# Inverted residual, odd blocks: second depthwise set ahead of the preceding block's output matmuls

## What is computed

```python
def _L3_conv_ref(x, w1, g1, b1, m1, v1, wd, gd, bd, md, vd, w2, g2, b2, m2, v2):
    HID, OUP = (288, 48)
    ...
    h = jnp.einsum('oc,bchw->bohw', w1, x)
    h = jax.nn.relu(_bn(h, g1, b1, m1, v1))
    h = jax.lax.conv_general_dilated(h, wd, window_strides=(1, 1), padding=((1, 1), (1, 1)), feature_group_count=HID, dimension_numbers=('NCHW', 'OIHW', 'NCHW'))
    h = jax.nn.relu(_bn(h, gd, bd, md, vd))
    h = jnp.einsum('oc,bchw->bohw', w2, h)
    h = _bn(h, g2, b2, m2, v2)
    return x + h
```

## Time and profile before

| what | before |
|---|---|
| median of 3 runs | 2010.66 us |
| range of the runs | 2002.27 to 2011.61 us |
| the profiled execution: its own time | 2013.56 us |
| the profiled execution: span in the trace | 2011.8 us |
| inverted residual within the span | from about 1545 us to the end |
| PE busy in the span | 1595.3 us, 79% |
| DVE busy in the span | 1479.1 us, 74% |
| ACT busy in the span | 1171.4 us, 58% |
| mean granted clock of PE in the span | 0.926 |

### The profile page before, as it was taken

The page is one execution under the profiler, slowest core; times in us unless marked ns, Lnnn a source line. Parts: engine busy times, 40 slices in busy tenths (PEclk is TensorE's granted clock), DMA queues, the critical chain, the costliest instruction groups (busy, mean ns, idle before and its releaser), DMA issues. The chain is left out here.

```text
span 2011.8 us, 41164 instructions
## 1 busy us (share of the span) xinstructions
PE 1595.3 (79%) x13002; PEld 940.3 (47%) x13002; DVE 1479.1 (74%) x2699; ACT 1171.4 (58%) x2257; POOL 637.3 (32%) x577
## 2 busy tenths in 40 slices
PE   6979418888888888803888888888860899999997
PEld 5545215555555555302555555555520344444444
DVE  5548858888888888654888888888856766666666
ACT  1115207888888888642888888888853434444341
POOL 2010015555555555302555555555500000000000
PEclk9999659999999999856999999999985799999999
DMA  2759356666666666565666666666576011011100
GB/s 64 251 201 217 93 135 105 107 106 107 107 108 107 107 106 103 97 144 130 106 107 106 108 106 107 106 106 107 85 119 161 15 34 34 21 31 34 34 18 25
DMA packets 132266, 199.40 MB, mean 99 GB/s; under 512 B 28528, under 2 KB 47824, under 8 KB 131920
## 3 DMA queue, kind: packets, MB, share of 16 engines
q1 hardware_dynamic: 132176, 198.08, 52.8%
HBM read 73.72 MB, written 37.75 MB: 55 GB/s over the span
## 5 line engine op out<-in xcount | busy, mean ns | idle before, releaser
L719 PE MATMUL gates_l<-xh_l,w_l 128*112 128x512 f32 x3072 | 801.2, 410 | 124.4 <-ACT xh_l L756 124.2
L719 PEld LDWEIGHTS gates_l<-xh_l,w_l 128*112 128x112 f32 x3072 | 502.8, 176 | 421.9 <-issue 286.5
L683 POOL TENSOR_TENSOR xh_l<-hs,xh_l 48x512 fp32r<-48x512 f32 x252 | 299.9, 1190 | 444.8 <-ACT xh_l L756 444.8
L692 POOL TENSOR_TENSOR xh_l<-xf_l,xs_l 48x512 fp32r<-48x512 f32 x256 | 307.1, 1200 | 47.8 <-DVE xs_l L825 47.4
L719 PE MATMUL gates_l<-xc_l,w_l 128*112 128x512 f32 x512 | 164.9, 403 | 143.0 <-DMA xc_l<-xs_l 135.8
L849 DVE TENSOR_TENSOR hs<-gate_o_l,tanh_c_l 48x256 f32 (+1 forms) x512 | 193.3, 416 | 73.9 <-ACT tanh_c_l L785 70.1
L1289 PE MATMUL b_dw<-b_hid,b_diag 32*32 32x512 f32 x6840 | 235.5, 601 | 0.0
L785 ACT ACTIVATE tanh_c_l<-cell_l 48x256 f32<-48x256 f32 x512 | 158.1, 342 | 99.2 <-DVE cell_l L840 99.2
L775 ACT ACTIVATE gate_if_l<-gates_l 112x512 f32<-112x512 f32 x256 | 151.3, 591 | 105.0 <-PE gates_l L719 101.8
L840 DVE TENSOR_TENSOR cell_l<-keep_l,gates_l 48x512 f32<-48x512 f32 x256 | 178.5, 697 | 26.6
L836 DVE TENSOR_TENSOR gates_l<-gate_if_l,gates_l 48x512 f32<-48x512 f32 x256 | 178.4, 697 | 22.3 <-ACT gates_l L779 1.0
(11 more groups left out here) (150 smaller groups left out, 1457.0 us busy)
## 6 DMA issues: line engine op xcount, KB each, us to landing
xc_l<-xs_l SPq DMA_DIRECT2D x512, 99.0 KB, 3.0
xh_l<-xs_l SPq DMA_DIRECT2D x512, 66.0 KB, 2.4
xf_l<-rows SPq DMA_DIRECT2D x256, 96.0 KB, 2.2
hs<-rows SPq DMA_DIRECT2D x32, 384.0 KB, 9.9
rows<-hs SPq DMA_DIRECT2D x32, 384.0 KB, 5.1
xr<-in_x_rows SPq DMA_DIRECT2D x24, 256.0 KB, 2.7
xc<-in_x_cols SPq DMA_DIRECT2D x24, 256.0 KB, 2.9
mixed<-stage SPq DMA_DIRECT2D x24, 256.0 KB, 3.0
```

The source lines that it names most:

```text
L683: pool.tensor_tensor(inner(xh[n:n + C, d, 1 - s, LO, :]), whole, inner(xh[n:n + C, d, 1 - s, HI, :]).bitcast(F32), ALU.subtract).then_inc( ...
L692: pool.tensor_tensor(inner(xh[f:f + C, d, s, HI, :]), wide(xf[f:f + C, s, :]), inner(x_rows(s, slice(f, f + C))).bitcast(F32), ALU.subtrac ...
L719: return nc.tensor.matmul(ps[d][m][0:K, :], w[:, d, q, m, :], padded(tile)[:, :, lo:lo + W], start=first, stop=last)
```

## The change

In odd blocks (those with both sets on PE, `not on_dve(k, 1)`), `reduce_main(k - 1, 0)` and `reduce_rest(k - 1, 0)` move from ahead of `expand(k + 2, 1)` to behind `depthwise(k, 1)`. On ACT `squash_v(k - 1)` moves from ahead of `squash(k, 0)` to just ahead of `squash(k, 1)`. Even blocks, DVE and SP stay as they were.

```diff
                     depthwise(k, 0)
                     if more:
                         expand(k + 2, 0)
-                    if k:
+                    if k and on_dve(k, 1):
                         reduce_main(k - 1, 0)
                         reduce_rest(k - 1, 0)
                     if more:
                         expand(k + 2, 1)
                     if not on_dve(k, 1):
                         depthwise(k, 1)
+                        reduce_main(k - 1, 0)
+                        reduce_rest(k - 1, 0)
                     if more:
                         expand(k + 2, 2)
                     if k:
...
                     if on_dve(k, 1):
                         begin_v(k)
-                    elif k:
-                        squash_v(k - 1)
                     squash(k, 0)
                     if more:
                         keep(k + 2, 0, (0, 1))
                         keep(k + 2, 1, (0, 1))
                     if not on_dve(k, 1):
+                        squash_v(k - 1)
                         squash(k, 1)
```

## The result

The changed kernel took 2032.11 us in the median of four runs (2031.12 to 2035.66), against 2008.38 us for the kernel before, now with a fourth run: 1.0121 times as long, with a 95% interval of 1.0095 to 1.0148. It is slower. The forecast was 2031.5 us. The sum hit the time, but two of its terms did not hit theirs; their errors cancelled. Part of the hit is the starting point too: the forecast was 20.8 us over a median of 2010.66 us, and the two medians measured lie 23.7 us apart.

What follows compares the result with a forecast made beforehand. The last quarter's stage was taken as bound by a chain passing from PE to ACT and back. Terms -0.4 + 13.1 + 11.6 - 3.5 = +20.8 us gave 2034.3 us profiled, 2031.5 us median; range 2016 to 2040.

Steps and rivals of the forecast that it cites:

- Which of the two arrives last in the first gap: Between an odd body's two sets, PE and ACT's copy arrive together, so output matmuls cost nothing; moving them gains 0.06 us.
- Rival D: First gap: output matmuls, not ACT's copy, hold expansion 1, so moving them gains; -11.2 us, 1999.5 us; chance 0.06.
- Term 2: Gap behind the second set of odd bodies grows from 6.84 to 8.7 us; +1.87 us times 7, +13.1 us.
- Term 3: First gap's new PE idle brings one clock fall per odd body, 7 x 1.65 = +11.6 us.
- Terms 1 and 3: Odd bodies: shorter first gap (-0.4 us) and clock falls in expansion 1 and second set (+11.6 us), together +11.2.
- the bound from block 0: Upper bound on the odd bodies' clock falls: block 0's slower expansion and next set, 2.98 us each, times 7 = 20.9.
- rival C: Low clock in odd bodies lasts as in block 0; +30.4 us, 2041 us; chance 0.09.
- The even bodies: Even bodies 2 to 12, set to set, were forecast unchanged, difference 0.
- rival E: Odd bodies fall, but even bodies lose their five clock falls; +12.5 us, 2023.2 us; chance 0.13.
- Term 4: Body 15: last set starts 7.8 us earlier, moved pair adds 2.6, one clock fall 1.65; sum -3.5 us.
- What was said to cost nothing: Odd bodies: `squash_v` moved behind ACT's copies, VectorE's `finish` some 11 us later, banks and output store following; no cost.

Runs made afterwards that it cites:

- the kernel with three fillers: Changed kernel plus three idle-filling matmuls between expansions 0 and 1 of every odd body: 2014.16 us against 2006.48 for the kernel before, ratio 1.0041.
- the ACT order put back: Changed order on TensorE alone; against the changed kernel, ScalarE's accumulator copy is first in the odd body again: 2040.16 us.
- the first experiment: Changed kernel plus four idle-filling matmuls between expansions 0 and 1 of every odd body: 2020.96 us.
- the last kernel of the study: Kernel before with the change in body 15 alone, half the second main output matmuls ahead of even bodies' expansion 2, block 0 fillers: 1989.23 us against 2006.96.

## Why the prediction was right, and where it was not

**Which of the two arrives last in the first gap**: right. Expansion 1 starts 3.74 us behind expansion 0, the number read from block 0. The output matmuls were free there, and taking them away freed nothing. Rival D fell with it.

**Term 2**, the second gap: right, +1.92 us per body against +1.87, +13.4 us in all. The step "the pair brings 2.64 and takes away the 0.75 of idle" is what the rows show; the kernel with three fillers shows it undisturbed by the clock (8.76 us again).

**Term 3**, the clock: the mechanism was right, shown by the two experiments that fill the first gap and by the ACT order put back; its size was wrong. The failed step is "I take 1.65 because block 0 had many more idle pieces before its set than the new gap has". Terms 1 and 3 together came to +21.0 us, not +11.2: 3.0 us per body, where the bound from block 0 was 2.98. The low clock went on for 6.7 us behind the idle in block 5, with PE busy in all of them, while in an even body of the kernel before it lasted 3.4. Block 0 was not only the upper bound but the nearer row: it has the same gap with the same idle, followed in both cases by an expansion at 2.08 us. I took the price from a fall behind half the idle. This was rival C's size, though not its wording: the low clock did not last as in block 0, where it stayed for some 17 us through four idle pieces, and that 2.98 meets 3.0 so closely is in part luck. Nor is block 0 always so: in the first profile of the changed kernel its expansion 1 ran at full clock behind the same 2.61 us, and the fall came one idle piece later.

```profile
1579.20 1.13 PE L1262 MATMUL b_ex<-b_xs,b_w1s 48*128 48x512 f32 x4 [2.61 <-ACT b_hid L1355]
```

The rule of the Trainium skill that I had set against this term (TensorE: Matmul & The Clock Gate, HAM oscillation) warns only of longer gaps than this one. What I had taken from it, that shorter ones cost nothing, the trace contradicts: all fourteen odd bodies in two profiles of the changed kernel ran at the low clock behind 2.61 us of idle.

**The even bodies**: wrong in the other direction. I had carried them unchanged, and gave 0.13 to their losing the five falls (rival E). They lost all five, 8.2 of the 8.8 us of that row. So the day went to C and E together, a pair of which I had priced each half alone: 30.4 - 8.3 = 22.1 us above the kernel before, against 21.5 measured in the stage. The forecast of 20.8 is as good a number for a wrong split, and that the two errors (+9.8 and -8.8 us) cancelled is luck. Neither the terms nor the chances had a case for both.

**Term 4**, the end: right, -3.7 against -3.5 us. The last set started 7.8 us earlier, as computed, and paid 1.48 us for the clock, where 1.65 was charged.

**What was said to cost nothing**: `squash_v` under the second set, VectorE's later `finish`, banks and stores. None shows in the trace: VectorE's first `finish` waits longer in odd bodies (23.2 us at most, against 15.8), and no PE row waits for it.

What stays open is why even bodies fall in one execution and are spared in another with the same instructions. The runs show that it repeated in two profiles of one kernel and that it changes with edits elsewhere. Where no idle piece of a body was over 0.75 us no fall was seen, with one exception: the filled gap of body 15 in the first experiment.

## What to carry to other kernels

Work that stands in the shadow of another engine is free only there: before moving it, look at how much shadow the new place has, here 0.75 us for 2.6 us of work. And such work does a second job, it keeps TensorE's clock up; the hole that it leaves was dearer here (21 us) than the place that it went to (13 us). When pricing a fall of the clock, take the row whose idle is as long as the new one, not the one that looks cleaner, and look at more than one execution: where and for how long the clock falls can differ between them.

## What the hardware showed that I had not expected

- The low clock can last much longer than the idle that it follows: 6.8 us behind 2.61 us of idle in the odd bodies, with PE busy in nearly all of them, and 3.4 us behind 1.37 us. The idle alone does not fix how long: behind the 2.60 us before the last set it was 3.4 us in the changed kernel and 6.8 us in the last kernel of the study.
- An idle of 1.37 us is followed by a fall in some executions and places and not in others, with the same instructions in the body (five of six bodies in the kernel before, three of six in the one that differs from it only in body 15, none in the changed kernel).
- A fall can come without any idle: behind four filling matmuls in body 15 of the first experiment, with PE busy all through the gap.
- Single matmuls of 48 by 128 weights on one half of the rows took about 0.9 us each, while a pair on the two halves takes 1.06 us together. Three of them in block 0 of the last kernel:

```profile
1575.84 2.73 PE L1302 MATMUL b_ys<-b_xs,b_w1s 48*128 48x512 f32 x6
```

Filling with such singles is coarse: four overshot a 2.6 us hole by 0.5 us.
